# Convolution taps multiplied into a projection (eight shifted products), with a new order in a linear-attention stage and a new unpacking of 4-bit weights

## The chip, the cores and the metric

The kernel runs on one core of one Trainium2 chip, as one launch, and everything is fp32. The metric is the device time of that launch in microseconds (us). Engines: PE is TensorE, DVE VectorE, ACT ScalarE, POOL GpSimd, SP the engine that only issues transfers here.

## The reference, cut to what matters

The program is a decoder of four layers on x of 32 x 64 x 256 (2048 tokens, 256 features). Each layer has three stages (a mixer, a second mixer, a feed-forward part), each behind a layer norm and added to x. The change touches three of the twelve stages.

```python
# L1_xattn: linear attention, 16 heads of 16; q from x, k and v from the context
f = lambda x: where(x > 0, x + 1, exp(x))
kv, den = sum_s f(k) v, sum_s f(k)
out = (sigmoid(x Wg + bg) * (f(q) kv) / (f(q) den + eps)) Wo

# L2_attn: state-space block, DI = 512 channels, N = 16 states, K = 4 taps
hs, gate = split(Win x)
hs = silu(causal_depthwise_conv(hs, Wconv, K = 4) + bconv)      # along the 64 steps
dt_in, B, C = split(Wx hs);  dt = softplus(Wdt dt_in + bdt)
h[t] = exp(A dt[t]) h[t-1] + dt[t] B[t] hs[t];  y[t] = sum_n C[t] h[t]
out = Wout ((y + D hs) * silu(gate))

# L2_ffn: gate, up (2048 x 256) and down (256 x 2048), weights packed in 4-bit codes
LUT = [0, .5, 1, 1.5, 2, 3, 4, 6, 0, -.5, -1, -1.5, -2, -3, -4, -6]
w = LUT[code] * scale[block of 32];  out = (gelu(x Wgate) * (x Wup)) Wdown
```

## The kernel before, in words

The stages run one after the other. x stays in SBUF as g.X (tokens on the partitions); a layer norm ahead of each stage writes its turned copy g.XT (features on the partitions). Tokens are worked in four chunks of CH = 512, or eight sequences of S = 64. Within a stage each engine has its own list of instructions, written out by hand, and waits on semaphores that the others raise; on one engine nothing overtakes. An fp32 matmul of 128x512 leaves two matmul records in the trace.

**Linear attention (`l1_xattn`).** A software pipeline over chunks n = 0 to 4: the new chunk's projections go through three PSUM banks `pr` as jobs Q0, Q1, G0, G1, K0 to K3 (L1225), `summary(n, j)` (L1240) multiplies keys and values of a tile of 128 tokens into `pkv`, DVE masks it (`mask`, L1367) and only then may the next summary be written. For the old chunk `attend(n-1, c)` (L1253) fills `pn` and `pd` for one half c of the features; DVE `denominator`, ACT `inverse` (L1330: Ln, Exp) and DVE `divide` (L1383) follow, and attend of the next half waits for that divide (`o_ready`), since pn and pd are one bank each. PE's order in a step is Q0, Q1, attend 0, G0, G1, attend 1, K0, K1, summary 0, project 0, K2, summary 1, project 1, K3, summary 2, summary 3. ACT runs inverse 0 behind G0, inverse 1 behind K0; DVE runs `gates` ahead of divide 0, and divide 1 behind the features of K0 and K1.

**State-space stage (`l2_attn`).** The scan is cut in 256 units u: chunk q = u // 64, state n and one of four channel blocks c. For each unit POOL multiplies `ub` (L1731), ACT makes `da` or, for four units, `dx` (exp of dt times A; two PSUM buffers, so unit u waits for the scan of u-2), DVE scans (L1793, L1798), DVE or, for 20 units of 64, POOL multiplies by C (`hc` L1802 with four buffers, `hp` L1720 with two), and PE adds it into `py` with an identity matmul (L1618). Beside the units run jobs, placed by unit number in `AT`: H (the hs projection of the next chunk, slots 2, 5, 8, 11), Z (the gate), S (the silus, between two table loads), X, D (dt) and O (output). `after` adds a lag for each engine: PE does H at its slot, ACT and DVE five units later. In H before, PE makes two matmuls (L1587), ACT copies them times the last tap into `acc` (L1638), and DVE adds the other three taps from PSUM, shifted by 1, 2 and 3 steps (L1757, three instructions and drains). All jobs share the two PSUM banks `pp`. In D, DVE computes max(x + bias, 0) into `mm0` (L1766), ACT log(1 + exp(-|x + bias|)) into `sa`, and POOL (for c*q of 2 and up) adds them and multiplies dtu. Ahead of the first unit, the first chunk runs H0 to H3, S, X0, D0, X1, D1 with nothing else beside it.

**Packed feed-forward (`l2_ffn`).** 8 blocks b of 256 hidden units, two passes h over the tokens. A unit is (b, i, n): gate and up for 512 tokens (8 matmul records, L1868), gelu by tanh on ACT and DVE (`inner`, `outer`), and `down` (4 records, L1877) two units later. In the first pass the weights of block b+1 are unpacked beside block b: DVE `codes` (4 instructions), ACT `parts` (2 of 128x1536), DVE `sizes`, `scales`, `weights` (4 of 128x1536, L1952 to L1963), one step behind each of the block's four units. PE waits for the whole of a block's weights (`w_ready`) ahead of its first unit.

Of the kernel before, what the change touches and what calls it, by code (L numbers as in the profile page):

```python
# [21 lines left out]
P = 128  # L22
# [5 lines left out]
CH = 512  # L28
# [1140 lines left out]
def l1_xattn(nc, g, a):  # L1169

    EPS = 1e-6
    with ExitStack() as ctx:
# [40 lines left out]
        with nc.Block() as block:  # L1213
# [8 lines left out]
            def _(pe):  # L1222
# [53 lines left out]
                for n in range(NCH + 1):  # L1276
                    new, old = n < NCH, n >= 1
                    if new:
                        job(n, "Q", 0)
                        job(n, "Q", 1)  # L1280
# [18 lines left out]
                    if new:  # L1299
                        job(n, "K", 3)  # L1300
                        summary(n, 2)
                        summary(n, 3)

            @block.scalar
            def _(act):
# [31 lines left out]
                for n in range(NCH + 1):  # L1337
                    new, old = n < NCH, n >= 1
                    if new:
                        job(n, "Q", 0)  # L1340
                        job(n, "Q", 1)
                        job(n, "G", 0)
                    if old:
                        inverse(n - 1, 0)
                    if new:
                        job(n, "G", 1)
                        job(n, "K", 0)
                    if old:
                        inverse(n - 1, 1)
                    if new:  # L1350
                        job(n, "K", 1)
# [4 lines left out]
            def _(dve):  # L1356
# [36 lines left out]
                for n in range(NCH + 1):  # L1393
# [14 lines left out]
                    if old:  # L1408
                        divide(n - 1, 1)
                    if new:  # L1410
# [14 lines left out]
def l2_attn(nc, g, a):  # L1425
# [6 lines left out]
    with ExitStack() as ctx:  # L1432
# [7 lines left out]
        w_loaded = s.sem("w_loaded")  # L1440
# [7 lines left out]
        layer_norm(nc, g, "2a", early=early)  # L1448
        hs = [s.sb(f"hs{k}", [P, IC, CH]) for k in range(2)]
# [4 lines left out]
        acc = s.sb("acc", [P, IC, CH])  # L1454
        sa = s.sb("sa", [P, 2, CH])
        mm0 = s.sb("mm0", [P, 2, CH])
# [8 lines left out]
        yy = s.sb("yy", [P, IC, CH])  # L1465
# [6 lines left out]
        (a_exp, pp0_free, pp1_free, raw_ready, tap_ready, conv_ready, hs_ready, z_ready, x_ready, dtin_ready,  # L1472
         bc_ready, bc_stored, d_ready, sp_ready, m_ready, dt_ready, dtu_ready, da_ready, ub_ready, scan_done,
         hc_ready, hp_ready, add_done, skip_done, zs_ready, yz_ready, o_ready) = s.sem(
            "a_exp", "pp0_free", "pp1_free", "raw_ready", "tap_ready", "conv_ready", "hs_ready", "z_ready",
            "x_ready", "dtin_ready", "bc_ready", "bc_stored", "d_ready", "sp_ready", "m_ready", "dt_ready", "dtu_ready", "da_ready",
# [70 lines left out]
        with nc.Block() as block:  # L1547
# [25 lines left out]
            def _(pe):  # L1573
                pe.wait_ge(w_loaded, nl)

                def job(q, j):
# [7 lines left out]
                    if kind in "HZ":  # L1584
                        oc = c if kind == "H" else IC + c
# [1695 lines left out]
```

## Time and profile before

| | us |
|---|---|
| median of 3 runs (lowest, highest) | 4644.61 (4644.49, 4649.68) |
| the profiled execution, device time | 4649.62 |
| its span | 4647.8 |
| PE busy | 3963.7 (85%) |
| DVE busy | 3130.9 (67%) |
| ACT busy | 2221.8 (48%) |
| POOL busy | 1510.8 (33%) |

All times in the text are counted from the start of the span. The three stages lie at about 604 to 770 (linear attention), 858 to 1455 (state space) and 1808 to 2188 (packed feed-forward). Three kinds of rows are shown below. A row of a window is: stretch, its length, then busy us and (x) number of instructions of PE, PEld (weight load), DVE, ACT and POOL, the granted TensorE clock as a share of 2.4 GHz, the DMA share and GB/s. A row of the timeline is: start, duration, engine, line, operation, tiles and shapes, xcount, and in brackets the idle time before it with what ended it. A row of a group of instructions is: line, engine, operation, tiles, shapes, xcount, then busy us and mean ns of one, then idle us before them.

### The profile page before, as it was taken

What the parts mean: (1) busy time and instruction counts of PE and PEld (TensorE: products, weight loads), DVE (VectorE), ACT (ScalarE), POOL (GpSimd) and SP (SyncE); (2) the same over time, 40 slices, a digit from 0 to 9 for tenths busy, and PEclk for the clock granted to TensorE, in tenths of its full rate; (3) what the DMA queues carried; (4) which work ended last, traced back from release to release, by engine and by line L of the source; (5) the groups of instructions that cost most, each with busy time, mean ns of one, the idle gap of its engine ahead of it and who ended that gap; (6) DMA issues with size and microseconds to landing.
All of it is one profiled execution on the core that took longest, in us unless ns stands there. A gap on an engine that the chain in (4) does not pass through costs nothing. (4 is left out here: it accounts for less than half of the span.)

```text
span 4647.8 us, 143172 instructions
## 1 busy us (share of the span) xinstructions
PE 3963.7 (85%) x62052; PEld 2603.5 (56%) x62052; DVE 3130.9 (67%) x5769; ACT 2221.8 (48%) x4151; POOL 1510.8 (33%) x1605
## 2 busy tenths in 40 slices
PE   7627886677767887999899999999999998689999
PEld 6515654323324775444576777777777776355555
DVE  7898935788887887754677777777777776521111
ACT  3446633554444554322566666666666665221111
POOL 1001200198894220000444344444444443112222
PEclk9859987888889998999899999999999999789999
DMA  1000000133332000000100000010010000041111
GB/s 35 19 27 11 2 13 21 61 121 112 125 133 69 2 2 28 28 0 10 43 26 22 22 25 22 22 26 22 22 29 22 22 13 4 7 136 54 53 50 44
DMA packets 72969, 175.13 MB, mean 38 GB/s; under 512 B 14578, under 2 KB 27892, under 8 KB 69748
## 3 DMA queue, kind: packets, MB, share of 16 engines
q1 hardware_dynamic: 72340, 165.96, 11.6%
q8 instruction: 490, 8.03, 0.7%
q14 instruction: 139, 1.14, 0.1%
HBM read 163.04 MB, written 2.88 MB: 36 GB/s over the span
## 5 line engine op out<-in xcount | busy, mean ns | idle before, releaser
L1731 POOL TENSOR_TENSOR ssm_ub<-ssm_dtu,ssm_bcn 128x512 f32<-128x512 f32 x256 | 324.6, 1295 | 299.5 <-DMA ssm_bcn<-ssm_bct 297.1
L3095 DVE TENSOR_TENSOR moe_hh<-moe_si,moe_pu 128x512 f32<-128x512 f32 x104 | 71.5, 688 | 450.5 <-PE moe_pu L2984 444.2
L2536 POOL TENSOR_TENSOR dn_gm<-dn_cb,dn_cs 128x256 f32<-128x256 f32 x128 | 76.8, 621 | 670.5 <-DMA dn_cb<-dn_cum 437.0
L3028 ACT ACTIVATE moe_si<-moe_pg 128x512 f32<-128x512 f32 x104 | 62.1, 597 | 467.2 <-PE moe_pg L2984 467.2
L1630 ACT ACTIVATE ssm_da<-core_XN,ssm_al 128x504 f32<-128x504 f32 x240 | 163.1, 683 | 252.1 <-DVE ssm_ph L1798 166.4
L2552 POOL TENSOR_TENSOR dn_eb<-dn_ee,dn_cc 128x512 f32<-128x512 f32 x64 | 66.7, 1042 | 651.8 <-DVE dn_cc L2662 651.8
L3047 POOL TENSOR_TENSOR moe_hw<-moe_hh,moe_cb 128x512 f32<-128x512 f32 x100 | 126.6, 1266 | 444.4 <-DVE moe_hh L3095 392.9
L1618 PE MATMUL ssm_py<-ssm_hc,core_ident 128*128 128x512 f32 x352 | 202.5, 679 | 65.5 <-DVE ssm_hc L1802 35.1
L2303 PE MATMUL dn_po<-dn_wo,dn_cT 128*128 128x256 f32 x1024 | 244.6, 393 | 2.4 <-ACT dn_cT L2470 2.2
L2218 PE MATMUL dn_pm<-dn_zz,dn_XB 32*32 32x32 f32 x16384 | 209.7, 194 | 29.3 <-issue 29.3
L2218 PEld LDWEIGHTS dn_pm<-dn_XB,dn_mb 32*32 32x32 f32 x16384 | 166.4, 105 | 111.8 <-issue 108.6
L1798 DVE TENSOR_TENSOR_SCAN ssm_ph<-ssm_da,ssm_ub 128x512 f32<-128x512 f32 x168 | 204.9, 1220 | 29.0 <-POOL ssm_ub L1731 16.6
L2303 PEld LDWEIGHTS dn_po<-dn_wo,dn_cT 128*128 128x128 f32 x1024 | 194.1, 194 | 30.8 <-ACT dn_cT L2470 3.3
L347 POOL TENSOR_TENSOR a_ke<-a_qkT,a_kmask 128x512 f32<-128x512 f32 (+1 forms) x96 | 84.6, 902 | 379.2 <-DVEq L637 303.3
L2218 PE MATMUL dn_pm<-dn_XB,dn_mb 32*32 32x32 f32 x16384 | 196.4, 194 | 9.3 <-issue 7.2
L2218 PEld LDWEIGHTS dn_pm<-dn_zz,dn_XB 32*32 32x32 f32 x16384 | 180.5, 103 | 34.9 <-issue 34.7
L2984 PE MATMUL moe_pg<-core_XT,moe_w 128*128 128x512 f32 x416 | 198.1, 599 | 0.0
L2984 PE MATMUL moe_pu<-core_XT,moe_w 128*128 128x512 f32 x416 | 195.5, 592 | 0.0
L2999 PE MATMUL moe_py<-moe_w,moe_hw 128*128 128x256 f32 x800 | 188.7, 379 | 0.0
L2999 PEld LDWEIGHTS moe_py<-moe_w,moe_hw 128*128 128x128 f32 x800 | 152.0, 190 | 62.5 <-issue 46.9
L560 ACT ACTIVATE a_sc<-a_sc 128x1024 f32<-128x1024 f32 (+1 forms) x128 | 121.5, 949 | 137.0 <-DVE a_sc L667 74.3
L2567 POOL TENSOR_TENSOR dn_mb<-dn_BD,dn_small 128x256 f32<-128x256 f32 x256 | 178.7, 734 | 0.0
(504 smaller groups left out, 10512.6 us busy)
## 6 DMA issues: line engine op xcount, KB each, us to landing
ssm_bcn<-ssm_bct SPq DMA_DIRECT2D x128, 512.0 KB, 3.7
dn_cb<-dn_cum SPq DMA_DIRECT2D x32, 512.0 KB, 4.9
dn_w<-in_dn_w SPq DMA_DIRECT2D x32, 388.0 KB, 3.5
moe_cb<-moe_rows SPq DMA_DIRECT2D x64, 192.0 KB, 2.9
moe_w<-in_moe_w SPq DMA_DIRECT2D x26, 384.0 KB, 7.3
moe_cb<-moe_rows SPq DMA_DIRECT2D x64, 128.0 KB, 3.0
dn_wo<-in_dn_w SPq DMA_DIRECT2D x16, 256.0 KB, 5.9
moe_cb<-moe_rows SPq DMA_DIRECT2D x64, 64.0 KB, 2.6
```

The source lines that it names most:

```text
L347: last = pool.tensor_tensor(dst[:, c, :, :], bcm(src[:, c, :], R), bc(kmask[:, :], P), ALU.mult)
L560: act.activation(flat(sc[par][:, 2 * h:2 * h + 2, :]), flat(sc[par][:, 2 * h:2 * h + 2, :]), ACT.Exp, scale=sl)
L1618: pe.matmul(py[:, turn_ % 2, :], g.ident[:, :], src[:, :], start=n == 0, stop=n == N - 1).then_inc(add_done, 1)
L1630: act.activation(nb(factor(u))[:, :, 1:S], nb(dt[q % 2][:, c, :])[:, :, 1:S], ACT.Exp, scale=al[:, n, c:c + 1]).then_inc(da_ready, 1)
L1731: pool.tensor_tensor(ub[u % NUB][:, :], dtu[q % 2][:, c, :], bcn[i % NB][:, 0, :], ALU.mult).then_inc(ub_ready, 1)
L1798: dve.tensor_tensor_scan(ph[:, m % 2, :], factor(u), ub[u % NUB][:, :], 0.0, ALU.mult, ALU.add).then_inc(scan_done, 1)
L2218: mm = pe.matmul(bank[r, n * HB:(n + 1) * HB], left(n, r), right(n, r), start=True, stop=True, tile_position=(q * HB, q * HB))
L2303: mm = pe.matmul(po[:, j // 2, (j % 2) * D:(j % 2 + 1) * D], cT[:, h * TPC + j, :], wo[e // NCH % 2][:, h, :], start=h == 0, stop=h == 1)
L2567: last = pool.tensor_tensor(halves(mb[i % 2][:, l - 1, :]), BD[:, :, :], bcm(small[:, 1 + l, :], NS), ALU.mult)
L2984: mm = pe.matmul(dst[:, m % 2, :], w[:, k, at:at + P], g.XT[:, kc, n * CH:(n + 1) * CH], start=kc == 0, stop=kc == DC - 1)
L2999: mm = pe.matmul(py[:, j, 0:D], h[:, j * P:(j + 1) * P], w[:, k, DC * 2 * P:], start=k == 0, stop=k == G - 1)
L3047: pool.tensor_tensor(hw[m % 3][:, :], hh[m % 3][:, :], cb[j % NCB][:, :], ALU.mult).then_inc(hw_ready, 1)
```

## The change

It is made of three edits.

Linear attention: summary 3 of a chunk moves behind Q0 of the next chunk on PE; ACT runs inverse 0 ahead of G0 and G1, and inverse 1 ahead of K0; DVE runs divide 0 and denominator 1 ahead of gates, and divide 1 ahead of the features of K0 and K1.

State space: `wt` holds three copies of the hs half of Win, each times one tap, and the last tap is multiplied into Win in place; the taps come by one broadcast transfer of 1 MB into `yy`. H is now eight matmuls into the same bank: two of 512 columns and six shifted ones that read and write eight runs of 63, 62 or 61 columns. DVE's part of H is gone, ACT copies the bank into `hs`. `acc` and `mm0` go; the max with 0 in D becomes a Relu on ACT in front of the Abs.

Packed feed-forward: a code is shifted so that its sign, exponent and mantissa bits lie where an fp32 has them, masked, and multiplied by 2^126 and the scale. All of it is on DVE, in three parts per block (gate, up, down), each with its own count of `w_ready`.

```diff
 # l1_xattn, PE
                     if new:
                         job(n, "Q", 0)
+                    if old:
+                        summary(n - 1, TPC - 1)
+                    if new:
                         job(n, "Q", 1)
...
                         summary(n, 2)
-                        summary(n, 3)
 # ACT
-                        job(n, "G", 0)
                     if old:
                         inverse(n - 1, 0)
                     if new:
+                        job(n, "G", 0)
                         job(n, "G", 1)
-                        job(n, "K", 0)
                     if old:
                         inverse(n - 1, 1)
                     if new:
+                        job(n, "K", 0)
 # DVE
                         denominator(n - 1, 0)
+                        divide(n - 1, 0)
+                        denominator(n - 1, 1)
                     if new:
                         gates(n)
                     if old:
-                        divide(n - 1, 0)
-                        denominator(n - 1, 1)
+                        divide(n - 1, 1)
                     if new:
                         features(n, "K", 0)
                         features(n, "K", 1)
-                    if old:
-                        divide(n - 1, 1)
 # l2_attn
+            sp.dma_start(flat(yy[:, :, :]), a["ssm_taps"][0:1, :].broadcast_to([P, K * DI])).then_inc(taps_loaded, 16)
...
 # PE
+                pe.wait_ge(wt_ready, 2)
...
+                    if kind == "H":
+                        straight = lambda kc: win[:, kc, c * P:(c + 1) * P]
+                        pe.matmul(out, straight(0), xt[:, 0, :], start=True, stop=False)
+                        for k in range(1, K):
+                            for kc in range(DC):
+                                pe.matmul(nb(out)[:, :, k:S], wt[:, K - 1 - k, kc, c * P:(c + 1) * P], nb(xt[:, kc, :])[:, :, 0:S - k],
+                                          start=False, stop=False)
+                        pe.matmul(out, straight(1), xt[:, 1, :], start=False, stop=True).then_inc(raw_ready, 1)
 # ACT, H and D
-                        act.activation(acc[:, c, :], out, ACT.Copy, scale=tap(K - 1, c)).then_inc(tap_ready, 1)
+                        if q >= 2 and c == 0:
+                            act.wait_ge(skip_done, IC * (q - 1))
+                        act.activation(hs[q % 2][:, c, :], out, ACT.Copy).then_inc(free, 1)
...
-                        act.wait_ge(m_ready, q * IC + c + 1)
+                        act.wait_ge(d_ready, q * IC + c + 1)
+                        if q * IC + c >= 2:
+                            act.wait_ge(dt_ready, q * IC + c - 1)
+                        act.activation(dt[q % 2][:, c, :], out, ACT.Relu, bias=tap(K + 2, c))
 # POOL
+                pool.tensor_tensor(wt[:, 0, :, :], win[:, :, 0:DI], bcm(taps[:, 0, :], DC), ALU.mult).then_inc(wt_ready, 1)
 # DVE
+                for k in range(1, K - 1):
+                    dve.tensor_tensor(wt[:, k, :, :], win[:, :, 0:DI], bcm(taps[:, k, :], DC), ALU.mult)
+                dve.wait_ge(wt_ready, 1)
+                dve.drain()
+                dve.tensor_tensor(win[:, :, 0:DI], win[:, :, 0:DI], bcm(taps[:, K - 1, :], DC), ALU.mult).then_inc(wt_ready, 1)
...
-                        for k in range(1, K):
-                            dve.scalar_tensor_tensor(dst[:, :, k:S], src[:, :, 0:S - k], tap(K - 1 - k, c), dst[:, :, k:S], ALU.mult, ALU.add)
-                            last = dve.drain()
...
-                        dve.tensor_scalar(mm0[:, c % 2, :], out, tap(K + 2, c), 0.0, ALU.add, ALU.max).then_inc(m_ready, 1)
-                schedule(job, unit, skip, {"H": 5, "D": 4, "O": 4})
+                schedule(job, unit, skip, {"D": 6, "O": 4})
 # l2_ffn, PE
+                        if t0 == 0 and n == 0:
+                            pe.wait_ge(w_ready, NW * b + c + 1)
...
+                    if h == 0 and i == 0 and n == 0:
+                        pe.wait_ge(w_ready, NW * b + 3)
...
-                            pe.wait_ge(w_ready, b + 1)
 # ACT: parts(b) is gone.  DVE: codes, sizes, scales and weights become
+                def weights(b, c):
+                    if c == 0:
+                        dve.wait_ge(pk_loaded[b % 2], 2 * NW * 16 * (b // 2 + 1))
                     for nib in range(2):
+                        dve.tensor_scalar(mi[:, nib, c, :], pk[b % 2][:, c, :], 28 - 4 * nib, 6, ALU.logical_shift_left, ALU.arith_shift_right)
+                    dve.drain()
+                    dve.tensor_scalar(mi[:, :, c, :], mi[:, :, c, :], CODE_BITS, None, ALU.bitwise_and)
                     dve.drain()
+                    dve.scalar_tensor_tensor(w[:, b, :, c, :], mi[:, :, c, :].bitcast(F32), CODE_UNIT, bcm(scl[b % 2][:, c, :], 2),
+                                             ALU.mult, ALU.mult).then_inc(w_ready, 1)
...
+                for c in range(NW):
+                    weights(0, c)
...
                         inner(k)
                         if h == 0 and b + 1 < NBLK:
+                            if 2 * i + n < NW:
+                                weights(b + 1, 2 * i + n)
```

## Rows read from the trace of the kernel before

**Rows 1.** State space: windows from scan to scan of 16 units.

```profile
903.02:939.42 36.40, 30.01 (x61) 12.32 (x62) 33.80 (x38) 15.37 (x24) 28.83 (x24) 0.88 0.35 119
1043.57:1081.83 38.26, 26.49 (x55) 11.80 (x56) 35.21 (x41) 13.13 (x21) 30.16 (x26) 0.87 0.32 112
1323.71:1353.64 29.93, 18.67 (x32) 6.69 (x33) 26.71 (x29) 10.65 (x17) 27.09 (x24) 0.83 0.38 128
1116.33:1155.71 39.38, 28.20 (x51) 10.54 (x49) 31.18 (x36) 19.87 (x30) 37.99 (x32) 0.83 0.37 125
```

**Rows 2.** State space, PE's timeline in the loop: jobs and units.

```profile
908.49 1.88 PE L1587 MATMUL ssm_pp<-core_XT,ssm_win 128*128 128x512 f32 x4
...
1050.26 3.81 PE L1618 MATMUL ssm_py<-ssm_hc,core_ident 128*128 128x512 f32 x4 [5.42 <-DVE ssm_yy L1783]
...
1058.71 1.88 PE L1587 MATMUL ssm_pp<-core_XT,ssm_win 128*128 128x512 f32 x4
1060.43 1.02 PE L1618 MATMUL ssm_py<-ssm_hp,core_ident 128*128 128x512 f32 x2
...
1086.31 3.62 PE L1604 MATMUL ssm_pp<-ssm_wout,ssm_yy 128*128 128x256 f32 x16
...
1100.79 4.58 PE L1593 MATMUL ssm_pp<-ssm_hs,ssm_wx 128*128 128x512 f32 x8
```

**Rows 3.** State space, the loop: the added taps on DVE, all 36.

```profile
L1757 DVE SCALAR_TENSOR_TENSOR ssm_acc<-ssm_pp,ssm_vec,ssm_acc 128x504 f32<-128x504 f32 (+2 forms) x36 | 26.3, 730 | 1.8
```

**Rows 4.** State space ahead of the first unit: timeline of PE and ACT.

```profile
871.28 3.67 PE L1587 MATMUL ssm_pp<-core_XT,ssm_win 128*128 128x512 f32 x8 [1.03 <-PEq L123]
...
883.14 2.56 ACT L1651 ACTIVATE ssm_hs<-ssm_acc,ssm_vec 128x512 f32<-128x512 f32 x4
...
889.41 0.60 ACT L1657 ACTIVATE ssm_dtin<-ssm_pp 128x512 f32<-128x512 f32 x1 [2.41 <-PE ssm_pp L1593]
```

**Rows 5.** Page: POOL's products and DVE's scans; DVE's timeline, one slow scan.

```profile
L1731 POOL TENSOR_TENSOR ssm_ub<-ssm_dtu,ssm_bcn 128x512 f32<-128x512 f32 x256 | 324.6, 1295 | 299.5 <-DMA ssm_bcn<-ssm_bct 297.1
L1798 DVE TENSOR_TENSOR_SCAN ssm_ph<-ssm_da,ssm_ub 128x512 f32<-128x512 f32 x168 | 204.9, 1220 | 29.0 <-POOL ssm_ub L1731 16.6
...
1093.89 2.22 DVE L1798 TENSOR_TENSOR_SCAN ssm_ph<-ssm_dx,ssm_ub 128x512 f32<-128x512 f32 x1
```

**Rows 6.** Linear attention: windows, the first and last of three steps.

```profile
623.89:661.98 38.09, 32.90 (x147) 21.24 (x145) 14.35 (x27) 9.58 (x22) 0.00 (x0) 0.91 0.00 1
...
701.19:740.23 39.04, 33.02 (x147) 20.49 (x145) 15.77 (x31) 9.70 (x22) 0.00 (x0) 0.91 0.00 1
```

**Rows 7.** Linear attention: timeline of PE and DVE in one step.

```profile
661.98 3.70 PE L1236 MATMUL lin_pr<-core_XT,lin_wq 128*128 128x512 f32 x8
...
669.03 3.65 PE L1236 MATMUL lin_pr<-core_XT,lin_wg 128*128 128x512 f32 x8
...
675.10 0.43 PE L1261 MATMUL lin_pn<-lin_qT,lin_kvm 128*128 128x64 f32 x2 [2.41 <-DVE lin_oT L1385]
...
681.10 6.26 PE L1233 MATMUL lin_pr<-lin_wkv,core_CT 128*128 128x512 f32 x8
...
700.13 1.13 PE L1249 MATMUL lin_pkv<-lin_vb,lin_kk 64*128 64x256 f32 x8 [1.48 <-DVE lin_kvm L1370]
```

**Rows 8.** Packed feed-forward: PE's timeline at blocks 0, 5 and 7.

```profile
1828.99 3.78 PE L1868 MATMUL nv_pg<-core_XT,nv_w 128*128 128x512 f32 x4 [12.16 <-DVE nv_w L1963]
...
1944.73 1.96 PE L1868 MATMUL nv_pg<-core_XT,nv_w 128*128 128x512 f32 x4 [1.74 <-DVE nv_w L1963]
...
1989.91 1.96 PE L1868 MATMUL nv_pg<-core_XT,nv_w 128*128 128x512 f32 x4 [1.74 <-DVE nv_w L1963]
```

**Rows 9.** Packed feed-forward, first pass: DVE's groups, and its first unpacking instruction.

```profile
L1975 DVE SCALAR_TENSOR_TENSOR nv_sq<-nv_sq,nv_pg 128x512 f32<-128x512 f32 x29 | 19.8, 683 | 1.5 <-ACT nv_sq L1924 0.7
L1968 DVE TENSOR_SCALAR nv_sq<-nv_sq 128x512 f32<-128x512 f32 x29 | 12.3, 424 | 29.4 <-ACT nv_sq L1922 29.4
...
1818.11 0.56 DVE L1946 TENSOR_SCALAR nv_mi<-nv_pk 128x768 int32<-128x768 int32 x1
```

More of the change, by code:

```diff
@@ L1439, in l2_attn @@
         vec = s.sb("vec", [P, K + 4, IC])
-        w_loaded = s.sem("w_loaded")
+        yy = s.sb("yy", [P, IC, CH])
+        taps = flat(yy[:, :, :]).rearrange("p (k c) -> p k c", k=K)
+        w_loaded, taps_loaded = s.sem("w_loaded", "taps_loaded")
         loads = [(win, "ssm_win"), (wx, "ssm_wx"), (wdt, "ssm_wdt"), (wout, "ssm_wout"), (al, "ssm_al"), (vec, "ssm_vec")]
@@ L1583, in job @@
                         pe.wait_ge(free, uses)
-                    if kind in "HZ":
-                        oc = c if kind == "H" else IC + c
+                    if kind == "H":
[6 more added lines that the diff above has]
+                        pe.matmul(out, straight(1), xt[:, 1, :], start=False, stop=True).then_inc(raw_ready, 1)
+                    elif kind == "Z":
                         for kc in range(DC):
-                            mm = pe.matmul(out, win[:, kc, oc * P:(oc + 1) * P], xt[:, kc, :], start=kc == 0, stop=kc == DC - 1)
-                        mm.then_inc(raw_ready if kind == "H" else z_ready, 1)
+                            mm = pe.matmul(out, win[:, kc, (IC + c) * P:(IC + c + 1) * P], xt[:, kc, :], start=kc == 0, stop=kc == DC - 1)
+                        mm.then_inc(z_ready, 1)
                     elif kind == "X":
@@ L1646, in job @@
                         if q < NQ:
-                            if q >= 2:
-                                act.wait_ge(skip_done, IC * (q - 1))
+                            act.drain()
                             for k in range(IC):
-                                act.wait_ge(conv_ready, q * IC + k + 1)
-                                act.activation(hs[q % 2][:, k, :], acc[:, k, :], ACT.Silu, bias=tap(K, k)).then_inc(hs_ready, 1)
+                                act.activation(hs[q % 2][:, k, :], hs[q % 2][:, k, :], ACT.Silu, bias=tap(K, k)).then_inc(hs_ready, 1)
                         act.preload_act_table_set("natural_log_exp_and_others")
@@ L1748, in _ @@
                 dve.drain().then_inc(a_exp, 1)
+                dve.wait_ge(taps_loaded, 16)
+                for k in range(1, K - 1):
[3 more added lines that the diff above has]
+                dve.tensor_tensor(win[:, :, 0:DI], win[:, :, 0:DI], bcm(taps[:, K - 1, :], DC), ALU.mult).then_inc(wt_ready, 1)
                 def job(q, j):
                     kind, c = j
[L1752 to L1766 removed]
+                    if kind == "D":
                         if q * IC + c < 2:
                             dve.wait_ge(sp_ready, c + 1)
[L1769 to L1770 removed]
+                            dve.tensor_tensor(dt[q][:, c, :], dt[q][:, c, :], sa[:, c, :], ALU.add).then_inc(dt_ready, 1)
                             dve.drain()
@@ L1840, in l2_ffn @@
         py = s.ps("py", [P, 2, DC, CH])
-        (code_ready, cst_ready, part_ready, sign_ready, scaled, w_ready, g_ready, u_ready, sq_ready, z_ready, th_ready,
-         done, sum_done, yt_ready, tt_ready) = s.sem(
-            "code_ready", "cst_ready", "part_ready", "sign_ready", "scaled", "w_ready", "g_ready", "u_ready", "sq_ready",
-            "z_ready", "th_ready", "done", "sum_done", "yt_ready", "tt_ready")
+        (w_ready, g_ready, u_ready, sq_ready, z_ready, th_ready, done, sum_done, yt_ready, tt_ready) = s.sem(
+            "w_ready", "g_ready", "u_ready", "sq_ready", "z_ready", "th_ready", "done", "sum_done", "yt_ready", "tt_ready")
         items = []
@@ L1858, in _ @@
                 for b in range(2, NBLK):
-                    sp.wait_ge(scaled, b - 1)
+                    sp.wait_ge(w_ready, NW * (b - 1))
                     codes_in(sp, b)
@@ L1895, in _ @@
                         _, h, b, i, n = items[k]
-                        if h == 0 and i == 0 and n == 0:
-                            pe.wait_ge(w_ready, b + 1)
                         gate_up(k, b, (2 * h + i) * CH, n)
@@ L1924, in _ @@
                         act.activation(sq[k % 2][:, :], sq[k % 2][:, :], ACT.Tanh, scale=0.7978845608028654).then_inc(th_ready, 1)
-                        _, h, b, i, n = x
-                        if h == 0 and i == 0 and n == 0 and b + 1 < NBLK:
-                            parts(b + 1)
                     else:
```

81 lines of the change are left out of this document (11 added, 70 removed).

## The prediction, made before the changed kernel ran

> **What bounds the kernel now.** The busy shares at the top of the page settle nothing: PE leads with 85%, but over twelve stages with different limits. So I read windows by stage first and then the timeline of the engine that ends each piece. In linear attention the three windows of a step last 38 to 39 us with PE busy 33 to 35 [rows 6]; the timeline of a step shows the idle places and the matmuls at half clock [rows 7]. In the packed stage PE starts with 12.16 us of idle and pauses 1.74 at the head of each block, both behind DVE's weights [rows 8]. In the state-space stage 16 units with H and Z beside them take 36 to 38 us, 16 units without an H take 29.93, and in neither is PE or DVE busy all the time; the last 16 units of a chunk are POOL's, 37.99 busy of 39.38 [rows 1]. All three edits touch what ends the wait in their stage. Two take waits off PE; the third gives PE work.
>
> **Linear attention: minus 28 us.** At full clock four records of 128x512 take 1.72 us (1058.71 to 1060.43), or 0.43 a record [rows 2]; half clock shows 0.86. A job has four, so eight jobs are 13.8. Two jobs and attend 0 together take 7.05 (661.98 to 669.03), so an attend is about 3.5. With four summaries of about 1.06 and two projections of about 0.9 a step's PE work is 13.8 + 7 + 4.2 + 1.8, about 28.8 with gaps. The step before takes 39. Of the difference, 2.41 is the wait for divide 0 ahead of attend 1 and 1.48 the wait for the mask ahead of summary 3; one of 0.74 is left. What follows the divide runs slowly: attend 1 takes 6.0 (675.10 to 681.10) for 3.5, and K0 and K1 6.26 for 3.5 [rows 7]. That is some 5.3 us of half clock, behind a pause.
> After the edit summary 3 stands behind Q0, and its mask (DVE is idle there) is done long before. The inverse of c = 0 no longer waits behind G0; inverse and divide, about 2 us, lie beside G0 and G1 (3.65). Gates move behind the divide, but DVE is busy only 14 to 16 of 39, so nothing on PE waits for them. With both waits gone I take the clock as full: step 28.9. Before, Q0 starts at 623.89, 661.98 and 701.19, and the last step ends at 740.23. After, the first of these starts 2.6 us sooner (a summary and its wait gone from the fill), then 28.9 each, so the last drain starts at about 711.95 where it was 740.23: minus 28.3. Bounds: minus 12.7 if the clock still falls once a step and its 5.2 us in three steps come back (15.6), minus 31 if the last pauses go too.
>
> **Packed feed-forward: minus 27 us.** Start: DVE begins at 1818.11 and PE at 1828.99. A part is now two shifts of 128x256 (half of the 0.56 for 128x768 [rows 9] would be 0.28 each), a mask of 128x512 at 424 ns and a scaled product of 128x512 at 683 ns [rows 9], so 1.7 to 1.8 with the drains. PE needs only the gate part: start at 1819.8, minus 9.2. The up part is there 1.8 us later, before four cold records end (3.78 [rows 8]). Blocks: from 1944.73 to 1989.91 is two blocks, 22.59 each, with 1.74 of pause in each [rows 8]. PE's work in one is four units of 12 records of 0.43, 20.6. DVE does 1.8 for a part and about 2.7 for inner and outer per unit of 5.15 us, so the parts are hidden, each of them a block ahead. The last block then begins near 1819.8 + 2 + 7 x 20.6 = 1966 (2 for the cold start), or 1962.8 by carrying the measured starts of the first blocks; I take 1962.8 to 1966 against 1989.91, so minus 24 to 27, and minus 27 as the term. ACT loses its two parts (it was not the bound). Bounds: minus 17 if only the start and half of the pauses are won, minus 28.
>
> **State space: plus 48 us.** A shifted matmul of 63, 62 or 61 columns times eight is 504, 496 or 488 columns, so by columns 0.42 a record. H was four records (1.72); it is now 4 + 12, or 1.72 + 5.0 = 6.7 us, five more per job and 80 over all sixteen. Where it lands:
> *Ahead of unit 0.* PE starts H0 at 871.28 [rows 4]. It must now wait for the products: the taps' megabyte (behind 2 MB of weights on the same queue) and then a 128x1024 product on POOL and three on DVE. POOL's 128x512 product is 1295 ns [rows 5], twice that is 2.6; DVE's 128x512 takes 683, about 1.2 for 1024. But both engines read SBUF with two inputs, and such a pair is slow: DVE's scan takes 1.22 as a rule and 2.22 with both inputs in SBUF and POOL active [rows 5]. 3.7 to 8 us after about 871; I take PE at 877.5. The page "SBUF — State Buffer" of the Trainium skill, section "SBUF: two separate sides", puts such a pair down to a shared port that one of them holds; by it alone DVE's and POOL's products would simply add up, 6.2 us, which is inside these bounds. Four H jobs are 26.8 us (2 more for the cold start), so H3 ends near 906; a copy, the table load, four silus (2.56 [rows 4]) and X0 follow, and dt_in, at 889.41 before [rows 4], comes at 912 to 914.5. I take plus 24.5. Before, PE did its four H early and DVE's adds (two thirds of this stretch) set the pace; that part is gone, so it is not 80/4 plus 6 but less by the lag of the adds. Bounds: plus 20 and plus 29.
> *In the loop*, chunks 1 to 3 are convolved beside units 0 to 16 of the chunk before. H0 starts 5.5 us after the first scan in the first chunk (908.49 less 903.02 [rows 1, 2]) and about 10 in the others. From there PE does 4 x 6.7 plus nine adds of 0.86 (34.6), and 3 x 1.72 for Z in the first chunk, without a pause, so H3 ends at +45.2. ACT copies it, and only then makes the decay of unit 16: the scan of unit 16 comes at +46.5, where it stands at 36.40 and 38.26 before [rows 1]: +10.1, +8.2, +8.2, about 26.5. DVE's taps (26.3 us over all 36, 730 ns each [rows 3]) and their drains leave: without them and without H a section takes 29.93 [rows 1], which would be 8.4 less each if PE were free; it is not. Output jobs (3.62 for sixteen records [rows 2]) fall behind this backlog, 0.7 twice.
> *In D* the maximum leaves DVE and a Relu of about 0.69 comes to ACT, which waited for that maximum before. The stretch is POOL's [rows 1], so 0 to minus 1 per chunk, 3 in all at most; I take 2. With more PE work ahead of X0 its eight records may run at full clock: 4.58 before against 3.44 [rows 2], and PE's pauses such as the 5.42 us at 1050.26 [rows 2] still come, so 1 per chunk and no more.
> Sum: 24.5 + 26.5 + 1.4 - 2 - 2, about plus 48; bounds plus 43 and plus 60.
> The page "SBUF — State Buffer" of the Trainium skill, section "Door 1: The DMA port swizzle (why [64,N] ≈ [32,N])", speaks against this edit: "any non-contiguous PSUM access pattern significantly slows down matmuls". No row here has such a matmul; without that sentence the price by columns stands.
>
> **Sum.** -28.3 - 27.1 + 48 = about -7. The profiled execution has 4649.62 (span 4647.8), 5.0 above the median; 4642.6 for its like, and 4644.61 - 7, about 4638, for the median. A measurement tells 0.2%, that is 9.3 us, from no change.
>
> **Rivals.**
> *A, the forecast*, -14 to 0: chance 0.40, of it 0.16 beyond -9.3 and 0.24 within.
> *B, the fuller PE keeps its clock.* For: half-clock records stand at 1050.26 and 1100.79 behind pauses [rows 2], and the backlog fills the first. Against: the D stretch stays POOL's. X0, the units beside it and the start of H at full clock are worth up to 3 a chunk, total -15: 0.22 (0.19 faster, 0.03 same).
> *C, shifted records cost more than their columns* (the other side). The path holds all 16 jobs of 12 shifted records, 192. Each 0.037 us more per record (9% of 0.43) gives 7 us, total 0; from +0.085 (20%) it is slower by over 0.2%; at the price of a half-clock record, 0.86, it adds 80, total +73, 4718. For: eight short runs in and out; against: DVE's 504 columns in runs of 63 show 730 ns against 683 for 512 whole [rows 3, 9], 7%, on another engine. By the page's sentence above it is this case, with its size not stated. 0.12 (0.03 same, 0.09 slower).
> *D, linear attention's clock does not come back*: +15.6, total +9: 0.08 (0.04, 0.04).
> *E, the edit to H is a gain because DVE, not PE, sets its sections*: each 29.9 instead of 46.5, total about -54. Against: the 34.6 us of PE work above. 0.05.
> *F, POOL's chain slips behind the longer H sections*, or the products take their 8 us: +8, total +1 to +10: 0.13 (0.08 same, 0.05 slower).
> Faster 0.16 + 0.19 + 0.05 = 0.40; same 0.24 + 0.03 + 0.03 + 0.04 + 0.08 = 0.42; slower 0.18. The likeliest case is 4638 in 4631 to 4645; the range 4620 to 4662 takes in B, D, F and the smaller prices of C, and leaves out E and the rest of C.
>
> **What would show it.** Linear attention: steps of 28.9 us, granted clock 1.0, no 2.41 idle. Packed stage: PE at 1.7 us behind DVE's first instruction, blocks 20.6 apart. State space: H's sixteen records in 6.7 us with PE behind the products by about 6; first scan 24 us later relative to the end of the stage before; the section of 16 units at 46.5 with PE full; D sections within a microsecond. Wrong would be: shifted records over 0.45, a linear step above 33, or an H section under 42 (then E holds).

## The result, and the profile after

| | us, or ratio |
|---|---|
| kernel before, median of 21 runs (lowest, highest) | 4647.46 (4635.08, 4653.93) |
| changed kernel, median of 21 runs (lowest, highest) | 4658.92 (4643.57, 4671.53) |
| ratio, 95% interval | 1.0028 [1.0019, 1.0037] |
| a second measurement of the changed kernel (12 runs) | 1.0015 [1.0003, 1.0026] |
| the kernel before measured against itself (12 runs) | 1.0000 [0.9987, 1.0014] |

The forecast was 7 us faster; the kernel is some 10 us slower, by 0.15 to 0.28%. First the page of the changed kernel, its span and busy times:

```profile
span 4662.3 us, 143470 instructions
PE 4033.0 (87%) x62244; PEld 2639.7 (57%) x62244; DVE 3059.8 (66%) x5738; ACT 2205.3 (47%) x4151; POOL 1515.9 (33%) x1606
```

DVE does 71 us less, PE is busy 69 us longer. Where the time went is read by stages. These are the windows of a step of linear attention, which answer to [rows 6]:

```profile
623.43:652.81 29.38, 29.38 (x147) 18.69 (x145) 14.31 (x28) 9.58 (x22) 0.00 (x0) 1.00 0.00 1
652.81:682.19 29.38, 29.38 (x147) 18.69 (x145) 14.44 (x30) 9.58 (x22) 0.00 (x0) 1.00 0.00 1
682.19:713.12 30.93, 29.45 (x146) 18.71 (x145) 15.84 (x32) 9.58 (x22) 0.00 (x0) 1.00 0.00 1
```

PE is busy without a gap and its granted clock is 1.00, where it was 0.87 to 0.91. The 1.48 us by which the third exceeds the others is the wait for the last mask, which has no next Q0 to hide behind. Next the packed stage, PE's timeline (at block 0 and block 7, as in [rows 8]), and then DVE's first unpacking:

```profile
1846.71 3.60 PE L1870 MATMUL nv_pg<-core_XT,nv_w 128*128 128x512 f32 x4 [2.88 <-DVE nv_w L1933]
...
1989.27 1.88 PE L1870 MATMUL nv_pg<-core_XT,nv_w 128*128 128x512 f32 x4
```

```profile
1844.87 0.50 DVE L1929 TENSOR_SCALAR nv_mi<-nv_pk 128x256 int32<-128x256 int32 x2 [0.30 <-PEq L123]
1845.45 0.43 DVE L1931 TENSOR_SCALAR nv_mi<-nv_mi 128x512 int32<-128x512 int32 x1
1845.96 0.69 DVE L1933 SCALAR_TENSOR_TENSOR nv_w<-nv_mi,nv_scl 128x512 f32<-128x512 f32 x1
```

PE starts 1.84 us behind DVE's first instruction (10.88 before [rows 8, 9]) and reaches block 7 after 142.56 us instead of 160.92. No pause is left at the head of a block: in PE's timeline the units start 5.15 us apart, and four units make a block of 20.6.

In the state-space stage the windows from scan to scan show PE as the bound where H runs. The first two are units 0 to 16 of the first and the second chunk, then come units 16 to 32 and 32 to 48 of the second (compare [rows 1]):

```profile
906.31:952.82 46.51, 44.50 (x102) 19.75 (x103) 25.68 (x27) 13.45 (x22) 27.28 (x23) 0.95 0.26 94
...
1057.13:1103.86 46.73, 41.17 (x92) 18.03 (x93) 26.79 (x30) 12.09 (x21) 28.63 (x25) 0.93 0.27 93
1103.86:1136.52 32.66, 30.12 (x86) 15.04 (x85) 28.23 (x28) 18.61 (x25) 29.66 (x22) 1.00 0.34 118
1136.52:1175.97 39.45, 27.94 (x51) 10.59 (x50) 28.40 (x31) 21.94 (x34) 38.06 (x32) 0.83 0.38 129
```

The chain from PE to the scans is in the list of waits of the window 1057.13 to 1103.86 (engine, who waits for whom, us in all, times, longest):

```profile
ACT ssm_hs L1649 <- PE ssm_pp L1593: 25.9, 4, 7.5
...
DVE ssm_hb L1799 <- ACT ssm_da L1639: 9.5, 2, 5.3
DVE ssm_ph L1804 <- ACT ssm_da L1639: 9.2, 2, 5.0
```

ACT waits 25.9 us for the four H jobs; the decays stand behind H in ACT's list, and DVE's scans wait 18.7 us for decays. An H job on PE's timeline, the first ahead of the loop and one in it:

```profile
854.14 2.05 PE L1588 MATMUL ssm_pp<-core_XT,ssm_win 128*128 128x512 f32 x2 [7.59 <-DVE ssm_win L1769]
855.98 7.22 PE L1591 MATMUL ssm_pp<-core_XT,ssm_wt 128*128 128x504 f32 x12
...
887.06 5.37 PE L1602 MATMUL ssm_pp<-ssm_hs,ssm_wx 128*128 128x512 f32 x8 [2.87 <-ACT ssm_hs L1660]
...
1067.43 1.48 PE L1588 MATMUL ssm_pp<-core_XT,ssm_win 128*128 128x512 f32 x2
1068.75 5.16 PE L1591 MATMUL ssm_pp<-core_XT,ssm_wt 128*128 128x504 f32 x12
1073.74 1.02 PE L1593 MATMUL ssm_pp<-core_XT,ssm_win 128*128 128x512 f32 x2
1074.60 1.02 PE L1627 MATMUL ssm_py<-ssm_hc,core_ident 128*128 128x512 f32 x2
```

All this is close to the forecast. Most of the rest is not in the changed stages. The table gives, for each profile, how many us longer a stretch took than in the profile of before that is shown ahead of the prediction. Each stretch runs from the first transposition of a layer norm to that of the next. The recurrent stage, which no edit touches, is cut in two: "head" runs from its first small matmuls to its first output matmul, "loop" from there to its last output. "lk" is what follows up to the next layer norm.

| profile | ahead of linear attention | linear attention and next | state space | packed | head | loop | lk |
|---|---|---|---|---|---|---|---|
| before, once more | 2.9 | -0.8 | -1.1 | -1.9 | 2.8 | -6.7 | 6.7 |
| changed | 1.3 | -25.9 | 51.1 | -27.7 | 12.1 | -4.8 | 7.3 |
| changed, once more | 1.3 | -26.4 | 48.0 | -27.8 | 9.0 | -8.7 | 6.9 |

Taken as means of two profiles each, the changed kernel's span is 8.35 longer: linear attention -25.75, state space +50.1, packed -26.8, which is -2.45 together; the head of the recurrent stage +9.15; lk +3.75, the loop -3.4, and 1.3 in four small places. The kernel before differs from itself by 6.7 us in the loop and by as much in lk, so of the unchanged stretches only the head stands clear of chance in these four profiles.

### The profile page after: what moved, and what is told of

Its sections match the earlier page's. It is cut to its first block and busy times, and to the rows that moved or that the text cites. A ratio compares the mean times of both kernels' runs of the same rounds, so it can differ in the third digit from the quotient of the medians.

```text
span 4662.3 us, 143470 instructions
## 1 busy us (share of the span) xinstructions
PE 4033.0 (87%) x62244; PEld 2639.7 (57%) x62244; DVE 3059.8 (66%) x5738; ACT 2205.3 (47%) x4151; POOL 1515.9 (33%) x1606
```

## The experiments

**Two edits without the third, and the third alone.** The sum over the stages says that the state-space edit costs what the other two win.

```diff
 # e1_lin_ffn: l1_xattn and l2_ffn changed
 # e2_ssm: l2_attn changed
```

> The kernel before with the linear-attention edit and the packed feed-forward edit, without the state-space one. By both theories the two stages give what they gave in the changed kernel's profile, about 26 and 28 us. Theory A (the time is the sum of the three changed stages, and the 15 us that the later stages lost in the changed kernel's profile are chance of one execution): 54 us less than before, ratio 0.9884, and the stages behind the packed one take what they took before within 3 us. Theory B (what PE waits for its own instructions at the head of the recurrent stage depends on how many instructions PE has been given before it): this kernel has another count than either, so these stages differ by any amount between 0 and about 15 us, and the ratio lies between 0.985 and 0.992.

Measured: 4593.45 us, ratio 0.9885 [0.9867, 0.9903]; in its profile linear attention is -25.9 and the packed stage -28.0, the head of the recurrent stage 88.5 us (88.1 before).

> The state-space edit alone. Both theories: the stage takes 51 us more, with the first scan 28 us later against the stage's own start and three sections of 16 units at 46.5 to 46.9 us. Theory A: +51, ratio 1.011. Theory B: +51 and 0 to 15 more from waits for instructions in the later stages, ratio 1.011 to 1.0143. A rival for the stage: beside the old linear attention the granted clock differs, and the stage takes less than 46.

Measured: 4700.99 us, ratio 1.0118 [1.0102, 1.0135], 55 us. The stage is +47.2, with the first scan 63.6 us behind the stage's first transposition (40.0 before) and sections of 46.76, 46.80 and 46.90. The head of the recurrent stage is +6.3. The sections were as expected, the first scan came 23.6 instead of 28 us later. The two ratios add up to 1.0003. So the edits add stage by stage, as far as ratios with intervals of 0.0018 tell; the changed kernel itself stands at 1.0028 and 1.0015. And the head grows with the state-space edit alone, which doesn't touch it.

**What the head of the recurrent stage waits for.** There PE does blocks of small matmuls of 32x32, 64 records each. Here are two of the four pauses in PE's timeline in the kernel before, and then two of the eight in the changed one; "issue" means that PE waits for nothing that the profile shows:

```profile
2270.35 0.61 PE L2218 MATMUL dn_pm<-dn_XB,dn_mb 32*32 32x32 f32 x48 [1.51 <-issue]
2271.46 0.33 PE L2218 MATMUL dn_pm<-dn_XB,dn_mb 32*32 32x32 f32 x16 [0.50 <-issue]
...
2272.30 1.98 PE L2195 MATMUL dn_bA<-core_XT,dn_w 128*128 128x512 f32 x4
```

```profile
2262.74 0.67 PE L2181 MATMUL dn_pm<-dn_zz,dn_XB 32*32 32x32 f32 x54
2265.40 0.26 PE L2181 MATMUL dn_pm<-dn_zz,dn_XB 32*32 32x32 f32 x8 [1.99 <-issue]
2265.59 3.00 PE L2158 MATMUL dn_bB<-core_XT,dn_w 128*128 128x512 f32 x4
...
2276.07 0.33 PE L2181 MATMUL dn_pm<-dn_zz,dn_XB 32*32 32x32 f32 x17 [2.12 <-issue]
2276.33 3.49 PE L2158 MATMUL dn_bA<-core_XT,dn_w 128*128 128x512 f32 x4
```

The second kernel stops in the middle of a block, 54 records in, for 2 us, and the four records of 128x512 behind such pauses take 3.00 and 3.49 us where they take 1.98: the granted clock is 0.64 and 0.55 there, for 1.00, so the pause costs once more. Of the 12.1 us by which the head is longer, 8.0 are such waits and 4.4 are PE busy for longer (73.59 us for 69.17). The same code gets the same data in both; it stands at another place in PE's instruction stream, since H gave PE 96 more matmuls. Two theories were put to the test. Theory A says that the time is the sum of the three changed stages and the rest is chance; theory B says that the waits depend on where the instructions stand in PE's stream. The test was made with waits on a semaphore long raised, at the end of PE's part of the packed stage, and by repeating both kernels.

```diff
+                for _ in range(128):
+                    pe.wait_ge(done, 1)
```

128 waits in the changed kernel, then in the one before, then both without any:

> The changed kernel with 128 further waits on a semaphore that has long been raised, as the last things that PE does in the packed stage, where it is idle for 5.9 us afterwards: they compute nothing. Theory A: up to 3 us slower than the changed kernel (what the waits cost beyond the idle time), the recurrent stage as before. Theory B: PE's instructions are moved by 128 against the places where it waits for the next ones, so the waits at the head of the recurrent stage (8 of 11.7 us in sum in the changed kernel, 4 of 3.7 us in the one before) change in number and place, and the time changes by several us either way; most likely down, by 5 to 12.

Measured: 4655.84 us, ratio 1.0012 [1.0003, 1.0022]. In its profile the head takes 92.7 us with 6 waits of 6.5: down, as theory B said.

> The kernel before with the same 128 waits in the same place. Theory A: 0 to 3 us slower than before, ratio 1.000 to 1.0006. Theory B: the waits for instructions at the head of the recurrent stage change here too; since before had few of them, most likely slower, by 3 to 15 us, ratio up to 1.003.

Measured: 4651.85 us, ratio 1.0010 [1.0000, 1.0019]. The head stays at 88.1 us, with 2 waits of 3.0: theory B's "most likely slower" did not come.

> The changed kernel once more, unaltered, for a second profile. Theory B (a stage's waits for instructions depend on the place of its instructions in PE's stream): the head of the recurrent stage, from its first small matmuls to the first output ones, again takes about 100 us (88 in the kernel before), with 8 waits of 11.7 us in sum, since the stream is the same. Theory A (chance of one execution): it is as likely to take 88 to 93 as 100. Ratio 1.002 to 1.0035.

Measured: 4652.91 us, ratio 1.0015 [1.0003, 1.0026]. The head is long again, 97.1 us with 7 waits of 10.0.

> The kernel before once more, unaltered. It shows how much two profiles of one program differ, stage by stage, and what ratio no change gives. Both theories: ratio 0.999 to 1.001. Theory B: the head of the recurrent stage takes 88 us again, and its loop, which was 5 to 10 us slower in the profile shown than in all the others so far, is slow again if that is a property of the stream, and not if it is chance.

Measured: 4646.54 us, ratio 1.0000 [0.9987, 1.0014]. The head takes 90.9 us with 4 waits of 4.0. The loop was not slow again (-6.7): that was chance of the one execution shown.

With 256 waits in the changed kernel:

> The changed kernel with 256 idle waits at the end of PE's part of the packed stage instead of 128. If the place matters by a period of 128 or 256 instructions, the head of the recurrent stage is again that of the changed kernel (100 us, 8 waits of 11.7 us), not that of the kernel with 128 (92.7). If it depends on the place in another way, the number lies anywhere from 88 to 100. Theory A: no relation, and 2 to 5 us are added for the waits themselves.

Measured: 4661.75 us, ratio 1.0036 [1.0024, 1.0048]; the waits themselves cost about 8 us here, as the packed stretch shows (-19.4 for -27.7). The head is 88.6 us and not 100 again, so the place does not matter by a period of 128 or 256 instructions.

With 384 waits in the kernel before:

> The kernel before with 384 idle waits at the end of PE's part of the packed stage: the changed state-space stage gives PE 96 matmuls more, each of which the trace shows as two matmul and two weight-load records, 384 in all. If the head of the recurrent stage is set by the sheer number of instructions that PE has been given, it is now that of the changed kernel in a kernel whose state-space stage is the old one: 97 to 100 us, 7 or 8 waits of 9 to 12 us. If not only the number counts (where the branches between stages stand, what the other engines fetch), it stays at 88 to 93 us with 2 to 6 waits. The idle waits themselves cost some 15 us beyond PE's idle time (128 cost 3, 256 cost 10), so the ratio lies at 1.003 if the head is unchanged and 1.005 to 1.006 if it isn't.

Measured: 4671.51 us, ratio 1.0050 [1.0030, 1.0070]. The waits themselves cost 15 us in the packed stretch; the head is 95.0 us with 6 waits of 6.3, longer than before but between the two outcomes expected.

The row of PE's waits for "issue" in the head (us in all, times, longest), first of the kernel before, then of the changed kernel and of its repetition:

```profile
PE dn_pm L2218 <- issue: 3.7, 4, 1.5
```

```profile
PE dn_pm L2181 <- issue: 11.7, 8, 2.3
```

```profile
PE dn_pm L2181 <- issue: 10.0, 7, 2.2
```

And of all kernels, those described below too:

| kernel | PE's stream up to here | waits for issue, us (times) | head, us |
|---|---|---|---|
| before; once more | H of two matmuls | 3.7 (4); 4.0 (4) | 88.1; 90.9 |
| two edits; with Relu | same H | 4.0 (4); 4.2 (4) | 88.5; 88.4 |
| changed, H cut to two | same H | 3.3 (3) | 88.7 |
| before, 128 idle waits | + 128 | 3.0 (2) | 88.1 |
| before, 384 idle waits | + 384 | 6.3 (6) | 95.0 |
| changed; once more | H of eight | 11.7 (8); 10.0 (7) | 100.2; 97.1 |
| state-space edit alone | H of eight | 9.0 (7) | 94.4 |
| changed, whole columns | H of eight | 10.0 (8) | 96.6 |
| changed, H spread | H of eight | 6.7 (6) | 92.6 |
| changed, 128; 256 idle waits | H of eight, + 128; + 256 | 6.5 (6); 4.4 (4) | 92.7; 88.6 |

The four programs with two matmuls in H and no idle waits wait 3.3 to 4.2 us, the four with eight 6.7 to 11.7, in repetitions too; idle instructions alone move it, up with the old state-space stage (6.3 with 384, though not with 128) and down with the new one (6.5 or 4.4). So the head's time depends on where PE's instructions stand in its stream. Theory A falls; of the kernels with idle waits there is one profile each, against differences of 2.8 and 3.1 us between two profiles of one program. The nearest test of the edit itself is the changed kernel with H cut to two: with only the six products of each H taken out, the head is back at 88.7 us. The guess that the number alone decides falls as well: 384 more waits in the kernel before give 95.0 us and 6.3, not 97 to 100 and 9 to 12, and with 256 the changed kernel doesn't return to its own pattern. The page "Runtime: NRT & Kernel Launch" of the Trainium skill, section "Instruction fetch mechanics", says that each engine's sequencer fetches its instructions in blocks by its own DMA queue and that this is hidden by the pace of issue. If the waits here are such fetches, they are not hidden behind runs of 32x32 matmuls: PE's row over the whole stage of the kernel before is

```profile
PE dn_pm L2218 <- issue: 36.5, 44, 1.6
```

But that they are fetches is argued and not shown. The queue that the profile calls "q8 instruction" moves 12 packets (0.20 MB) in the head of either kernel, with 4 waits or with 8, and of the 32 waits of 0.9 us and more in the whole stage of the kernel before only 6 overlap one of its transfers. Nor do the waits grow over the whole stage: the same row is 37.5 us in the second profile of the kernel before, and 38.2 and 30.7 in the two of the changed kernel. How they fall to the head is what differs.

**Is it DVE or PE that sets the sections with H?** This kernel leaves out the products with the earlier taps. In this diff and the next, long lines are joined and the index of `wt` is cut to `...`.

```diff
-                        for k in range(1, K):
-                            for kc in range(DC):
-                                pe.matmul(nb(out)[:, :, k:S], wt[...], nb(xt[:, kc, :])[:, :, 0:S - k], start=False, stop=False)
```

> The changed kernel with the six shifted products of each H job left out (the taps before the last one then count for nothing): H is two matmuls, and DVE has no taps either. Theory of the prediction (PE's 6.7 us per H job sets the 16 units with H, and 26.8 us ahead of the first unit): these sections fall from 46.5 to about 30, as the one without an H, and the first scan comes 20 us sooner; the stage takes about 70 us less than in the changed kernel, and 19 less than before. Rival (POOL and the hand-over of buffers set these sections, and DVE's relief is worth nothing): they stay at 36 to 38, and the stage ends within 5 us of before's less the taps ahead of the first unit.

Measured: 4579.61 us, ratio 0.9848 [0.9827, 0.9868]. The windows of units 0 to 16 of its first two chunks:

```profile
888.66:916.74 28.08, 26.07 (x54) 11.21 (x55) 25.38 (x27) 13.64 (x22) 27.10 (x23) 0.86 0.43 152
1021.49:1051.44 29.95, 24.47 (x50) 9.96 (x49) 26.71 (x29) 12.53 (x21) 27.11 (x24) 0.86 0.35 127
```

28.1 and 29.95 for 46.5 and 46.7, the first scan 47.9 us behind the stage's start for 67.9, and the whole stretch -17.7 against before, 69 less than in the changed kernel. So the taps on DVE lengthened a section by 8 us, as reckoned, and on PE they lengthen it by 17 to 18. The rival of POOL falls.

**Do short runs cost more than their columns?**

```diff
-                                pe.matmul(nb(out)[:, :, k:S], wt[...], nb(xt[:, kc, :])[:, :, 0:S - k], start=False, stop=False)
+                                pe.matmul(out, wt[...], xt[:, kc, :], start=False, stop=False)
```

> The changed kernel with its six shifted products done over all 512 columns, unshifted and in one run, so the result of the convolution isn't the reference's. By columns alone an H job is 6.88 us instead of 6.71, and the stage 2 to 3 us longer. Rival (runs of 61 to 63 columns with gaps cost more than their columns): the stage is shorter than the changed kernel's by anything above 2 us.

Measured: 4650.18 us, ratio 1.0012 [0.9997, 1.0027]; the stage +55.1 against before, 4.0 and 7.1 longer than in the two profiles of the changed kernel, sections 48.73, 47.63 and 47.32 for 46.5 to 46.9. The shifted form is the cheaper one in the stage. The whole kernel is no slower for it, since its loop, which the edit leaves alone, takes 1675.7 us here for 1688.8 and 1692.7; why was not found. The changed kernel's tile view says the same of single records (lowest, median, highest ns):

```profile
L1591 PE MATMUL ssm_pp<-core_XT,ssm_wt x192: 571/578/1047, 856.0 to 1247.8; 128*128 128x504 f32 x64, 128*128 128x496 f32 x64, 128*128 128x488 f32 x64
```

578 for 488 to 504 columns, 592 for 512. The page "SBUF — State Buffer" of the Trainium skill, section "Door 1: The DMA port swizzle (why [64,N] ≈ [32,N])", warns of any non-contiguous pattern in PSUM; with runs of 61 to 63 fp32 the measurement shows no such cost.

**PE's sum, or the deadline of H?**

```diff
-        AT = {("H", 0): 2, ("H", 1): 5, ("H", 2): 8, ("H", 3): 11, ("O", 0): 14, ("O", 1): 17, ("S", 0): 20, ("X", 0): 23,
-              ("X", 1): 25,
+        AT = {("H", 0): 2, ("H", 1): 7, ("H", 2): 12, ("H", 3): 17, ("O", 0): 20, ("O", 1): 23, ("S", 0): 22, ("X", 0): 25,
+              ("X", 1): 28,
```

> The changed kernel with H at units 2, 7, 12 and 17, the silus at 22, X at 25 and 28, and output at 20 and 23. Theory 1 (PE's sum over units 0 to 32 is what counts: 74 us of work in 79 to 84): the first section falls to 38 to 42, the second rises, and the two together gain 1 to 4 us a chunk, 3 to 10 in all. Theory 2 (the backlog only counts because the silus' slot stands so early): 7 or more a chunk, 20 in all, and the changed kernel would then be level with or below before. Rival: the later X and output jobs run into D, and it gets slower by up to 10.

Measured: 4642.01 us, ratio 0.9990 [0.9978, 1.0002]. Its windows of units 0 to 16 and 16 to 32 of the second chunk:

```profile
1055.24:1091.46 36.22, 30.66 (x66) 13.30 (x67) 26.62 (x30) 11.15 (x18) 27.53 (x24) 0.91 0.32 108
1091.46:1130.94 39.48, 39.48 (x109) 19.68 (x108) 27.78 (x30) 19.73 (x28) 31.96 (x24) 1.00 0.34 117
```

75.70 for the two, 79.39 in the changed kernel (72.76 before): PE is now the bound of the second window, busy in all of it. The three chunks gain 3.8, 3.7 and 4.6, the stage is 13.8 shorter than in the changed kernel's profile and 37.3 longer than before. The gain of 12 in all lies a little above the 3 to 10 of theory 1 and well under the 20 of theory 2: the backlog's early deadline cost about 4 us a chunk, PE's additional work the rest. That the kernel is level with before was expected of theory 2 alone; its head, 92.6 us for 97 to 100, gives part of that, and no edit here was aimed at it.

**The Relu without the products.**

> The kernel before with the linear-attention edit, the packed edit, and of the state-space edit only the Relu on ACT in place of DVE's maximum. The stretch of D is POOL's: 0 to 3 us less than the kernel without the Relu, ratio 0.988 to 0.9885. Rival (ACT's six instructions of D get in the way of the decays): 3 to 8 us more. The waits for instructions at the head of the recurrent stage stay at about 4 us, since PE's stream is that of the kernel with the two edits.

```diff
 # on top of the two edits
-                        dve.tensor_scalar(mm0[:, c % 2, :], out, tap(K + 2, c), 0.0, ALU.add, ALU.max).then_inc(m_ready, 1)
+                        act.activation(dt[q % 2][:, c, :], out, ACT.Relu, bias=tap(K + 2, c))
```

Measured: 4586.71 us, ratio 0.9874 [0.9857, 0.9891], which can't be told from 0.9885 without it; the D windows are 39.43, 39.42 and 39.41, as before. The stage is 3.1 us longer than without the Relu, 2.6 of it in units 16 to 32 of the second chunk, which take 34.5 or 31.7 us in two profiles of the kernel before as well. The Relu is worth nothing that shows, and the kernel with two edits, with or without it, is the best that computes the reference: 54 to 58 us less than before.

## Why the prediction was wrong

*Linear attention, minus 28.3*: -25.8, right in its mechanism and 2.5 too large. Both waits and the half clock are gone; a step is 29.38 and not 28.9 (PE's own work is that long), three times, and the last step has its mask wait of 1.48.

*Packed stage, minus 27.1*: -26.8. The start gained 9.0, the blocks 18.4. Blocks of 20.6 and the hidden parts are as worked out.

*State space, plus 48*: +50.1 in the mean of two. Ahead of unit 0 it is +27.9 and +24.3 in the two profiles (24.5 forecast); of the difference 1.5 is how long the cold clock lasts over the first H (7.22 or 5.71 for its twelve records) and 1.7 is X0 at half clock in one of the two (5.37 for its eight records, or 3.67). PE starts 7.5 us later than before against the stage's start (6.2 forecast); the products take 6.4 us from POOL's start at 847.63 to DVE's last end at 853.99, so most of the excess lies ahead of them. The sections are 46.51, 46.73 and 46.86 for 46.5. Units 16 to 32 of the second and third chunk take 32.7 with the clock at 1.00 in both profiles. The kernel before has 34.5 and 34.6 at 0.89 and 0.90 in the profile shown, but 31.7 and 33.7 at 1.00 and 0.95 in its second, and in the first chunk they gain nothing; so the fuller PE brings 1.6 us in all in the means. D is 39.45 for 39.38, so the Relu's 2 us did not come.

*Rivals*: B, up to 3 us a chunk, came as 1.6 in all. C falls by the whole-column run, D by the clock of 1.00, E by its sections of 46.5 to 46.9, where it needed 29.9 (its total should have read -57: three sections 16.6 shorter than in the forecast). F is half there: the products cost 7.5 of its 8, but POOL's sections stayed at 39.45.

*The sum is the step that failed.* "About -7" took every stage without an edit as unchanged, without a reason for it. The three terms came out at -2.45 together, 5 above their sum of -7.4 and inside their bounds; that alone would still have been a gain. Then the head of the recurrent stage, 700 us after the state-space stage has ended, takes 9.15 more, since H's 96 further matmuls move PE's stream: that turns the gain into a loss. The row was there to be read before: of all PE's matmuls those of this stage had the largest total of waits for issue, 36.5 us. I did not ask what more instructions on PE do to code that follows.

*What stays open.* The means of all runs are 4656.5 (33 runs of the changed kernel) and 4646.4 (106 of before), 10.1 apart, with some 3 us of uncertainty; -2.45 and +9.15 make 6.7. The loop and lk differ by up to 7 us between two executions of one program, so two profiles a side can't place the last 3 us. Over the five profiles with two matmuls in H and the five with eight, all without idle waits, the head is 88.9 and 96.2 us in the mean, 7.3 apart and without overlap, and the loop 1689.7 and 1687.7. So the head's share is nearer 7 than 9, and 3 to 7 us of the whole difference are not placed. And what it is about the stream that decides (its number, where the branches between stages stand, what the other engines do) was not found, nor what the waits for issue wait for.

## What to carry to other kernels

An operation that moves to the engine that is nearly full there costs its whole duration there, however much it frees elsewhere: 5 us more a job on PE against 2.2 less on DVE. Before moving work, ask for each window what the receiving engine already does, and how early its result is due. This kernel's long runs of tiny matmuls changed their time with the instruction stream ahead of them, so in a kernel with such runs a difference of a quarter of a per cent needs a repetition, a padded variant and the stage-by-stage table before it is put down to the edit. And edits that act in separate stages should be measured apart: here two are worth 1.2% and the third takes all of it back.

## What the runs showed of the hardware

PE's waits for issue in the head of the recurrent stage are 0.2 to 2.3 us long, and some are followed by matmuls at half clock, as shown above. Idle waits on a raised semaphore take PE some 7 us per 128, or 55 ns each: its pause behind the packed stage is 9.1 us with 128 of them, 16.1 with 256 and 22.9 with 384.

The lk stretch has two times, 7 us apart, in one and the same program. These are PE's timelines there in the kernel before, in its repetition, and in the changed kernel:

```profile
4022.15 1.13 PE L2754 MATMUL lk_py<-lk_wo,lk_mr 128*128 128x256 f32 x4 [2.79 <-DVE lk_mr L2844]
...
4028.89 3.70 PE L2744 MATMUL lk_pp<-core_CT,lk_wi 128*128 128x512 f32 x8
```

```profile
4017.04 1.13 PE L2754 MATMUL lk_py<-lk_wo,lk_mr 128*128 128x256 f32 x4 [2.87 <-DVE lk_mr L2844]
...
4021.34 2.07 PE L2754 MATMUL lk_py<-lk_wo,lk_mr 128*128 128x256 f32 x4
...
4027.65 6.32 PE L2744 MATMUL lk_pp<-core_CT,lk_wi 128*128 128x512 f32 x8
```

```profile
4029.45 1.13 PE L2717 MATMUL lk_py<-lk_wo,lk_mr 128*128 128x256 f32 x4 [3.17 <-DVE lk_mr L2807]
...
4031.13 2.08 PE L2717 MATMUL lk_py<-lk_wo,lk_mr 128*128 128x256 f32 x4
...
4040.59 5.76 PE L2707 MATMUL lk_pp<-core_CT,lk_wi 128*128 128x512 f32 x8
```

The pause of 2.79 us is followed by full clock, those of 2.87 and 3.17 by half clock for some 15 us. In all fourteen profiles of this text it goes that way: five have 2.75 to 2.83 us there, full clock and 74.8 to 75.1 us for the stretch, nine have 2.87 to 3.17, half clock and 81.4 to 82.1. Both kinds stand on both sides, and the kernel before showed both, so no edit is behind it. Whether the length of the pause decides, or something that only goes with it, no run here tells.

Ahead of the loop, DVE's small scaling of `al` (128x64) took 2.10 us beside POOL's product, for 0.20 in the kernel before, where POOL was idle. The first row is POOL's, in POOL's timeline, the second DVE's, in DVE's:

```profile
847.63 2.34 POOL L1751 TENSOR_TENSOR ssm_wt<-ssm_win,ssm_yy 128x1024 f32<-128x1024 f32 x1 [240.90 <-POOLq L123]
```

```profile
847.92 2.10 DVE L1758 TENSOR_SCALAR ssm_al<-ssm_al 128x64 f32<-128x64 f32 x1 [0.64 <-ACT ssm_al L1634]
```
